# Transposing x for the attention of blocks 1 to 4 through DRAM scratch and VectorE instead of on TensorE, in a one-core Macaron layer

## The reference

```
x = x + 0.5 * ffn(layernorm(x))      # FFN 1
x = x + attention(layernorm(x))
x = x + 0.5 * ffn(layernorm(x))      # FFN 2

ffn(z):  z_prev = z shifted by one token in its sequence
         r = sigmoid((mu_r*z + (1-mu_r)*z_prev) @ W_r.T)
         k = (mu_k*z + (1-mu_k)*z_prev) @ W_k.T
         return r * (square(relu(k)) @ W_v.T)
attention(z): q = relu(z@Wq.T)/4; k = relu(z@Wk.T)/4; v = z@Wv.T; u = silu(z@Wu.T)
         per head: kv = k.T @ v over the whole sequence; o = q @ kv
         return (rmsnorm_per_head(o) * u) @ Wo.T
```

## Time and profile before

| | |
|---|---|
| median of the runs | 307.89 us |
| the profiled execution | 307.94 us, of which the span of the trace is 306.2 us (1.74 us lie outside) |
| PE busy | 298.5 us, 97% of the span |
| DVE, ACT, POOL busy | 81%, 77%, 70% |
| granted clock of PE | full in all 40 slices |
| DMA | 15.05 MB; 17122 of 28416 packets under 512 B |

### The profile page before, as it was taken

The page is one execution under the profiler, slowest core; times in us unless marked ns, Lnnn a source line. Parts: engine busy times, 40 slices in busy tenths (PEclk is TensorE's granted clock), DMA queues, the critical chain, the costliest instruction groups (busy, mean ns, idle before and its releaser), DMA issues.

```text
span 306.2 us, 5777 instructions
## 1 busy us (share of the span) xinstructions
PE 298.5 (97%) x2003; PEld 271.7 (89%) x2003; DVE 247.4 (81%) x601; ACT 235.5 (77%) x461; POOL 214.5 (70%) x237
## 2 busy tenths in 40 slices
PE   6999999999999999999999999999999999999995
PEld 4888879978988898998988998999999999999894
DVE  4899896677876966985993798596989798999695
ACT  3988949969779779689178368489797979699981
POOL 4598969779689489479168116736797979759823
PEclk9999999999999999999999999999999999999999
DMA  7950070070330510000000000000001101001123
GB/s 234 382 208 2 2 137 2 2 137 0 58 83 0 80 59 0 2 1 2 0 2 1 2 0 0 2 2 2 0 16 56 37 34 54 17 2 68 42 99 137
DMA packets 28416, 15.05 MB, mean 49 GB/s; under 512 B 17122, under 2 KB 27364, under 8 KB 28388
## 3 DMA queue, kind: packets, MB, share of 16 engines
q1 hardware_dynamic: 28096, 14.42, 16.7%
q10 hardware_dynamic: 292, 0.26, 0.2%
HBM read 8.39 MB, written 6.29 MB: 48 GB/s over the span
## 4 chain that ended last, share of the span: by engine, by line
PE 63%; DVE 16%; POOL 8%; ACT 7%; issue 3%; DMA 1%; ACTq 0%; DVEq 0%; POOLq 0%
PE psK L1328 6%; PE psX L1328 6%; PE psK L1330 6%; PE psK L1329 6%; PE psX L1330 6%; PE psX L1329 6%; PE psRV L1328 5%; PE psRV L1330 5%; PE psRV L1329 5%; DVE mix L978 3%; PE psA L1533 2%; PE psX L1546 2%; PE psK L1533 2%; PE psA L1345 2%; DVE gate L1054 2%
## 5 line engine op out<-in xcount | busy, mean ns | idle before, releaser
L978 DVE SCALAR_TENSOR_TENSOR mix<-psA,mu,mix 128x512 f32<-128x512 f32 x60 | 41.5, 744 | 10.0 <-ACT mix L663 10.0
L454 POOL TENSOR_TENSOR mix_k_lo<-mix,mix_k_hi 128x512 fp32r<-128x512 f32 x26 | 33.6, 1313 | 5.1 <-ACT mix_k_hi L696 5.1
L663 ACT ACTIVATE mix<-psA,one_mu 128x511 f32<-128x511 f32 x60 | 36.9, 697 | 0.0
L1328 PE MATMUL psRV<-ffn_hi,mix_r_hi 128*128 128x256 f32 x120 | 34.3, 286 | 0.0
L1330 PE MATMUL psRV<-ffn_hi,mix_r_lo 128*128 128x256 f32 x120 | 33.6, 280 | 0.0
L1329 PE MATMUL psRV<-ffn_lo,mix_r_hi 128*128 128x256 f32 x120 | 33.5, 279 | 0.0
L646 ACT ACTIVATE xn<-xs,shiftA,rstdA 128x256 f32<-128x256 f32 x53 | 27.9, 623 | 2.6 <-POOL shiftA L438 2.6
L1328 PE MATMUL psRV<-ffn_hi,act_hi 128*128 128x256 f32 x96 | 27.6, 287 | 0.2 <-POOL act_lo L476 0.2
L1330 PE MATMUL psRV<-ffn_hi,act_lo 128*128 128x256 f32 x96 | 26.8, 279 | 0.0
L1329 PE MATMUL psRV<-ffn_lo,act_hi 128*128 128x256 f32 x96 | 26.8, 279 | 0.0
L947 DVE BATCH_NORM_STATS2 statsA<-xs 128x6 f32<-128x256 f32 x64 | 22.4, 412 | 2.7 <-DMA xs<-x_dram 2.6
(11 more groups left out here) (211 smaller groups left out, 1086.5 us busy)
## 6 DMA issues: line engine op xcount, KB each, us to landing
xs<-x_dram SPq DMA_DIRECT2D x7, 512.0 KB, 7.8
out_dram<-xs SPq DMA_DIRECT2D x7, 512.0 KB, 2.8
spread<-xn SPq DMA_DIRECT2D x8, 256.0 KB, 4.5
squares<-spread SPq DMA_DIRECT2D x8, 256.0 KB, 2.7
out_dram<-xs SPq DMA_DIRECT2D x4, 128.0 KB, 1.7
xs<-x_dram ACTq DMA_DIRECT2D x2, 128.0 KB, 3.1
xs<-x_dram SPq DMA_DIRECT2D x2, 128.0 KB, 2.8
silu_u<-w_ffn_k_dram SPq DMA_DIRECT2D x1, 256.0 KB, 4.0
```

What stands on the lines that cost most here:

```text
L454: nc.gpsimd.tensor_tensor(mix_k_lo[:, h, :], mix[:, 0, h, :], mix_k_hi[:, h, :].bitcast(F32), ALU.subtract).then_inc(s_lo_k, 1)
L663: nc.scalar.activation(mix[:, rk, h, 1:BLOCK], psA[:, h, 0:BLOCK - 1], ACT.Copy, scale=one_mu[:, rk, h:h + 1]).then_inc(s_prev, 1)
L978: nc.vector.scalar_tensor_tensor(out=m, in0=psA[:, h, :], scalar=mu[:, rk, h:h + 1], in1=m, op0=ALU.mult, op1=ALU.add).then_inc(s_mix, 1)
L1328: nc.tensor.matmul(dst, a_hi, b_hi, start=start, stop=False)
```

## The change

Four things, all in stages 1 to 6:

1. The transposes of x for attention blocks 1 to 4 (`TURNED_X`) leave PE. SP stores x after FFN 1 from `xs` to a second scratch `spread_x` in pieces of 32 floats, loads it into `gout` (free at that time), and DVE turns it with `turn_x` into psX. The xn store now writes pieces of 128 floats, since ACT writes xn with the 32x32 blocks already in the scratch's order.
2. ACT does `x2_high(a)` between the two halves of `activate_k(i)` in stages 2 to 5. PE's `k_and_u` waits for each half of x2 by itself.
3. `stats_a` of blocks 5 to 7 moves one stage ahead: its four bn_stats stand before the four silus, and its bn_aggr behind `stats_b`. `keep_g` stands before `r_low`.
4. In stage 1 ACT squares act_k's second half instead of POOL; in stage 2 the split of wo stands a little earlier on POOL and ACT.

```diff
+        TURNED_X = range(1, 5)
+        quads_x = gout[:].rearrange("p t d -> p (t d)")
+        spread_x = nc.dram_tensor("spread_x", [len(TURNED_X), 2, QUADS, P, P], F32).ap()
...
-            for k, n in enumerate(TURNED):
+            for k, (n, a) in enumerate(zip(TURNED, TURNED_X)):
                 for g in range(2):
+                    sp.wait_ge(s_x1, 2 * a + g + 1)
+                    sp.dma_start(spread_x[k, g].rearrange("j p (q f) -> p q j f", f=QUAD),
+                                 row(xs, a, g * BANK, BANK).rearrange("p (q j f) -> p q j f", j=QUADS, f=QUAD)
+                                 ).then_inc(s_spread_x[g], 16)
+
                     sp.wait_ge(*normalized(n, 2 * g + 1))
-                    sp.dma_start(spread[k, g].rearrange("j p (q f) -> p q j f", f=QUAD),
-                                 xn[:, 2 * g:2 * g + 2, :].rearrange("p t (h j f) -> p (t h) j f", h=HALVES, j=QUADS)
+                    sp.dma_start(spread[k, g].rearrange("j p e -> p j e"),
+                                 xn[:, 2 * g:2 * g + 2, :].rearrange("p t d -> p (t d)").rearrange("p (j e) -> p j e", j=QUADS)
                                  ).then_inc(s_spread[g], 16)
                 if k > 0:
+                    sp.wait_ge(s_tB, 2 * a)
                     sp.wait_ge(s_tA, 2 * n)
                 for g in range(2):
+                    sp.wait_ge(s_spread_x[g], 16 * (k + 1))
+                    sp.dma_start(quads_x[:, g * BANK:(g + 1) * BANK],
+                                 spread_x[k, g].rearrange("j (c i) e -> (j c) (i e)", i=QUADS)).then_inc(s_quads_x[g], 16)
                     sp.wait_ge(s_spread[g], 16 * (k + 1))
...
-                activate_k(i)
-                if a is not None and i > 1:
+                if a in TURNED_X:
+                    activate_k(i, (0,))
+                    x2_high(a)
+                    activate_k(i, (1,))
+                else:
+                    activate_k(i)
+                if i > 5:
                     x2_high(a)
...
+            def turn_x(a):
+
+                dve.wait_ge(s_relu_q, 2 * a)
+                blocks = quads_x.rearrange("p (g i t h f) -> p g h t i f", g=2, i=QUADS, t=2, h=HALVES)
+                for g in range(2):
+                    dve.wait_ge(s_quads_x[g], 16 * (a - TURNED_X[0] + 1))
+                    for h in range(HALVES):
+                        last = nc.vector.transpose(
+                            psX[:, h, half(g)].rearrange("p (t c i) -> p t i c", t=2, i=QUADS), blocks[:, g, h, :, :, :])
+                        if g == 1:
+                            last.then_inc(s_tB, 1)
...
             for i in range(1, 7):
+                if i == 2:
+                    stats_a(4)
                 if 1 < i <= 5:
-                    stats_a(i + 2)
                     turn(i + 1, {4: [(s_wcen, 4)], 5: [(s_kvbd, 1)]}.get(i, ()))
+                if i - 1 in TURNED_X:
+                    turn_x(i - 1)
...
-                            pe.wait_ge(s_x2hi, 2 * a + HALVES)
-                            pe.wait_ge(s_x2lo, 2 * a + HALVES)
+                            pe.wait_ge(s_x2hi, 2 * a + c + 1)
+                            pe.wait_ge(s_x2lo, 2 * a + c + 1)
...
                 ffn_k(i, [(s_gacc, i - 1)])
-                transpose_b(i - 1)
                 ffn_r(i)
```

More of the change, by code:

```diff
@@ L170, in macaron @@
         s_quads = [sem(f"s_quads_{g}") for g in range(2)]
+        s_spread_x = [sem(f"s_spread_x_{g}") for g in range(2)]
+        s_quads_x = [sem(f"s_quads_x_{g}") for g in range(2)]
         s_prev = sem("s_prev")
@@ L465, in act_squares @@
                 for h in range(HALVES):
+                    if (n, h) == (1, 1):
+                        continue
                     pool.wait_ge(s_act_hi, parts(n) + h + 1)
@@ L566, in _ @@
                     kt_low(i - 1)
+                if i == 2:
+                    pool.wait_ge(s_wo_hi, 1)
+                    nc.gpsimd.tensor_tensor(wo_lo[:], wo[:], wo_hi[:].bitcast(F32), ALU.subtract).then_inc(s_wo_lo, 1)
                 scales_b(i)
@@ L645, in normalize @@
                         continue
-                    nc.scalar.activation(xn[:, t, :], tile_row(xs, b, t), ACT.Identity,
+                    given, rows = tile_row(xs, b, t), xn[:, t, :]
+                    if n in TURNED:
+                        given, rows = given.rearrange("p (h j f) -> p h j f", h=HALVES, j=QUADS), spread_rows(t)
+                    nc.scalar.activation(rows, given, ACT.Identity,
                                          bias=shiftA[:, t:t + 1], scale=rstdA[:, t:t + 1]).then_inc(s_xn, 1)
@@ L713, in activate_k @@
                     nc.scalar.activation(act_hi[:, h, :], act_k[:, h, :], ACT.Square).then_inc(s_act_hi, 1)
+                    if (n, h) == (1, 1):
+                        act.wait_ge(s_act_hi, HALVES)
+                        nc.scalar.activation(act_k[:, h, :], act_k[:, h, :], ACT.Square).then_inc(s_act_first, 1)
             def activate_k2(n):
@@ L848, in _ @@
                     nc.scalar.activation(wo_hi[:], wo[:], ACT.Identity).then_inc(s_wo_hi, 1)
+                x1_high(i)
                 relu_q(i - 1)
@@ L1220, in _, with projections @@
             ffn_weight_low(2)
-            def projections(a):
+            def projections(a, n=None):
                 for t in range(TILES):
+                    if n is not None:
+                        bn_rows(n, (t,))
                     silu(a, t)
             for i in range(1, 7):
+                if i == 2:
+                    stats_a(4)
                 if 1 < i <= 5:
-                    stats_a(i + 2)
                     turn(i + 1, {4: [(s_wcen, 4)], 5: [(s_kvbd, 1)]}.get(i, ()))
+                if i - 1 in TURNED_X:
+                    turn_x(i - 1)
                 if i > 1:
@@ L1234, in _ @@
                     stats_a(3)
-                projections(i - 1)
+                projections(i - 1, i + 3 if 2 <= i <= 4 else None)
                 if i == 6:
@@ L1244, in _ @@
                 stats_b(i)
+                if 2 <= i <= 4:
+                    bn_all(i + 3)
+                keep_g(i - 1)
                 r_low(i + 1)
@@ L1247, in _ @@
                     center_weight("v", 4)
-                keep_g(i - 1)
                 if i == 4:
@@ L1627, in _ @@
             ffn_k(5, [(s_gacc, 4)])
-            transpose_b(4)
             ffn_r(5)
```

11 lines of the change are left out of this document (6 added, 5 removed).

## The result

The changed kernel takes 326.2 us (median of four runs, 324.28 to 327.31) beside 307.97 us for the kernel before on the same chip: a ratio of 1.0559 [1.0516, 1.0601], 5.6% slower. The profiled execution has a span of 324.7 us. The direction was as forecast, the size was not: 317.0 us was predicted, and 326.2 lies above the range.

A forecast was written before the change was run, and what follows sets the result against it. PE, busy 97% of the span, bounds the kernel; its 4.7 us saving lies inside the wait for x. Span 306.2 plus 9.1 (x 6.5 late, k_lo 2.6) is 315.3, with 1.74 outside 317.0 us; range 310.3 to 322.5.

The forecast's parts named there:

- T: The moment x after FFN 1 of a block is complete, at the end of the second add_ffn1.
- L: Way from T through store and load to the last load's landing: 7.6 us, bounds 6.0 to 9.4.
- 2.06 + 1.72 + 11.8: Loop after L: DVE's transposes 2.06 us, ACT to the column of previous 1.72, from there to the next T 11.8.
- then the load takes 2.7 us: Last step of L: the load behind the store lands 2.7 us later.
- the queue chokes: Rival: small-piece stores hold SP, L is 9 us or more, result 322 us and up; chance 0.02 beyond 9.4.
- T of stage 1: Start of the sum: T in stage 1 falls at 40.2 us, 40.61 before the change.
- Three turns: Three rounds from T to T at 23.2 us each, bringing stage 4's T to 109.8 us.
- T of stage 4 to k_and_u of stage 5: From T in stage 4 to the start of stage 5's k_and_u: 10.7 us, reaching 120.5.
- The wait for k_lo: In stage 5 POOL's k_lo comes 2.6 us late for gram; longer turns hide this in stages 2 to 4.
- Only POOL is late: Rival: x2 in time, act_hi's half 1 1.0 us later behind x2_high, k_lo eats 0.8 us a stage; 307 us; chance 0.06.
- PE keeps its gain: Rival: PE stays the bound in the stages and keeps its saving; 303.2 us, some 304; chance 0.10.
- keep_g ahead of r_low: Removes PE's stop for g_acc and smaller ones at other stages' ends; 1.0 us together.

The follow-up runs named there:

- e4: e3 plus all stores and loads of x through DRAM, which nobody uses until long after; 311.6 us.
- e8: e3 plus the stores of x, without any load of x; 307.9 us.
- e13: Changed kernel without the loads of x; its stores and all orders stay, and DVE turns whatever lies in gout; 319.8 us.
- e5: Changed kernel without stores and loads of x, and with ACT's old order (both halves of activate_k, then x2_high); 305.9 us.
- e2: Changed kernel without the stores and loads of x; DVE's transposes and ACT's new order stay; 311.6 us.
- e7: e1 with loads issued x, x, xn, xn and DVE's turn_x ahead of turn(i+1); 311.1 us.
- e3: Changed kernel with PE transposing x again, no x through DRAM and ACT's old order; the other edits stay; 306.6 us.
- e1: Changed kernel with ACT's old order: x2_high behind both halves of activate_k; 322.2 us.
- e6: Changed kernel with ACT writing xn in its old layout and the xn store in pieces of 32 floats; 329.5 us.
- e10: e1 with DVE's turn_x ahead of turn(i+1), load order as in the changed kernel; 313.2 us.
- e11: e1 with loads issued x, x, xn, xn, DVE's order as in the changed kernel; 323.5 us.
- e9: e3 with xn's old layout and the xn store in pieces of 32 floats; 307.0 us.
- e12: e7 with ACT's new order, x2_high between the halves of activate_k; 314.3 us.

## Why the prediction was right in kind and wrong in size

**Right: which resource would set the time.** The forecast said that all that PE saves lies inside a wait for x, and that this wait stands in ACT's program and closes a loop through the next T. The chain of after is that loop. A turn is L + 15.6 us by the forecast's steps (2.06 + 1.72 + 11.8); measured, the turns of 24.8, 25.6 and 24.9 us less their L of 9.1, 9.9 and 9.25 leave 15.7, 15.7 and 15.65. PE does stop 3.08, 1.52 and 2.32 us before k_and_u in stages 2 to 4 (not in stage 5, where a stop was forecast, too).

**Wrong: the step "then the load takes 2.7 us" in L.** SP's queue in stage 3's turn, beside the earlier trace rows:

```profile
66.57 1.59 SPq L405 DMA_DIRECT2D spread<-xn  x1
68.29 0.45 SPq L413 DMA_DIRECT2D gout<-spread_x  x1
...
70.54 0.32 SPq L416 DMA_DIRECT2D squares<-spread  x1
```

The last load is issued at 70.54 and landed at 75.82, with three loads of the same size ahead of it, the first 2.25 us earlier. Issue (0.67 us to the last store's, forecast 0.65) and store (3.96, forecast 4.25) were right or better; the load was 5.28, and 4.40 and 4.62 in the other two turns. I had priced the neighbours of the stores and left the loads at the median of a trace that never had more than two in the queue. The range's long end (9.4) had the same fault. Of the rival "the queue chokes" the length came true, L of 9 or more, and I gave such times 5% (0.03 and 0.02); its mechanism did not, for the last store was issued 0.67 us after T, where 0.65 was forecast. e4, e8 and e13 show by themselves that adding the loads of x costs the time, e4 and e8 on a kernel that does not even use them.

How a queue of four makes the last load slow is only half answered. Windows of after from the issue of that load on, and the queue of instruction transfers in the half microsecond from 72.50 (packets, MB, share of 16 engines):

```profile
70.54:73.50 2.96, 2.96 (x15) 2.45 (x14) 1.45 (x4) 1.28 (x3) 2.96 (x2) 1.00 0.87 269
73.50:75.80 2.30, 2.30 (x17) 2.11 (x16) 0.00 (x0) 1.15 (x2) 1.15 (x2) 1.00 0.04 9
```

```profile
q8 instruction: 1, 0.02, 22.3%
```

In the last 2.3 us before the load lands the DMA engines are nearly idle (share 0.04, 9 GB/s). Just before that, between 72.50 and 73.00, a transfer of instructions of 16 KB (queue q8) has started. Such a transfer starts inside each of the slow last loads of after; in the fourth trip, where that load took 3.46 us, it starts only 0.3 us before the landing. Over all 15 traces 27 of the 184 loads of `squares` and `gout` took over 4.4 us, and every one has such a transfer starting inside it, among them three with at most one more load in the queue (5.16 us in e5, 4.93 in e13's third trip, 4.44 in e8). The 87 loads without one took 2.8 us (median) and 4.36 at most. No run moved these transfers, so that they cause the delay is not shown, and how L's excess divides between them and the queue stays open.

**The sum, term by term** (spans, 324.7 measured and 315.3 forecast, 9.4 apart):
- T of stage 1, 41.13 for 40.2: 0.9. It belongs to the start-up, which is 1.3 us later in this trace than in that of before and as early as there in that of e13.
- Three turns, 75.3 for 69.6: 5.7. L accounts for 5.4 of it.
- T of stage 4 to k_and_u of stage 5, 12.5 for 10.7: 1.8. Here x was in time. turn(i+1) waits in this stage for kv_bd, which comes behind kv(0) and so behind the late gram (DVE's kv_bd 123.57, its transposes 124.03), and PE reached k_and_u without an idle. I had taken it that k_lo's lateness in stages 2 to 4 is hidden by the longer turns; in stage 4 it is not.
- From there to the end, 195.8 for 194.8: 1.0. In stage 5 gram starts 138.31 - 128.93 = 9.4 us behind k_and_u, where it was 8.3, and runs 5.22 us for 2.82: together 3.5 us late, where 2.6 were forecast. The wait for k_lo was priced, the clock behind it not.

**Half right: the rivals.** "Only POOL is late" was priced at the 0.8 us per stage that PE gains. e2 shows the mechanism with x in time: 5.6 us (e2 less e5), more than all that PE gained, since act_hi's second half was queued not only behind 1.0 us of x2_high but behind the transposes of psA and psX that x2_high waits for. "PE keeps its gain" would need trips of no length, and e5, which has none, gains 0.7 to 2.5 us of the 3.2 in the runs and nothing in the stages of its trace. So the transposes were not worth the whole 0.79 us a stage that the issue distance says: in e5's trace POOL's k_lo and once xn's load take their place.

**Right: the rest.** keep_g ahead of r_low was given 1.0 us and measures 1.05. The Trainium skill's "VectorE: DVE Perf Modes", "Rules for kernel authors", would leave 128x128 transposes on TensorE; here DVE's way gains at most a little when the trips cost nothing (e5), and with trips its best order still costs over 4 us (e7 beside e3). The runs agree with the rule.

## What to carry to other kernels

Price a new transfer by where it stands in the queue: the last of four loads took 3.5 to 5.3 us where loads took 2.7 before, and a load that nobody waits for delayed the one that somebody did. In an engine's program, look at what stands behind the new wait, and put the wait that is needed first in front: two lines of DVE's program swapped gave back 9 us, nearly three times the 3.2 us of the transposes. An engine at 97% is not proof that a us off it is a us won; an experiment that grants the new path for nothing (here: turning whatever lies in the buffer) shows about the most that the new path can bring.

## What the runs showed of the hardware that I had not expected

**PE's clock.** The granted clock was full in all 40 slices before. In the stages of after, e1, e2, e6, e7, e10, e11 and e13 it falls to 1.2 GHz, and each time PE stands idle or has just done so; in those of e3, e4, e5, e8, e9 and e12 it stays full. Windows of gram in stages 2 and 5 of after, which follow stops of PE for k_lo of 1.82 and 0.95 us and have another of 0.65 us inside:

```profile
63.81:69.11 5.30, 4.66 (x24) 4.45 (x25) 4.01 (x15) 2.40 (x5) 4.06 (x5) 0.68 0.86 160
...
138.31:143.53 5.22, 4.56 (x24) 4.36 (x25) 3.75 (x11) 1.86 (x4) 2.75 (x3) 0.70 0.02 5
```

The 24 matmuls take 5.3 and 5.2 us there (5.2 in stage 4, too). In stage 3 they take 3.82 us, with a stop of the same kind inside but at full clock, so some 1.4 us are the clock's. In e1 the drop comes in the first half of k_and_u. Its first and last such window:

```profile
54.97:60.02 5.05, 5.05 (x13) 3.95 (x13) 4.23 (x9) 4.85 (x10) 2.07 (x3) 0.53 0.00 0
...
128.76:131.61 2.85, 2.85 (x12) 2.33 (x13) 2.40 (x4) 2.85 (x6) 1.36 (x3) 1.00 0.00 0
```

The same twelve matmuls take 5.05 and 2.85 us. PE had stood idle 4.00 us before the first and 2.57 before the last, but the length of that idle alone does not decide: in e7 idles of 1.78 us were followed by clocks of 0.69 and 0.61, and one of 2.23 us by 1.00; in e10 3.31 us was followed by 1.00. What does decide stays open. A wait of PE here cost its own length and, often but not always, 1.1 to 2.4 us more (k_and_u's first half takes 3.98 to 5.26 us, the longest in e6 and e11, instead of 2.85).

**SP's issue.** The second xn store of a turn, in pieces of 128 (128x4x128), holds SP 1.59 us, where stores in pieces of 32 held it 0.67 and 1.02 before. The larger pieces are not the reason: in e2, with the same xn stores and no x stores before them, each holds SP 0.37 us and lands in 2.2 us, while in e9, with pieces of 32 and no x stores, they hold it 0.59 to 1.83 us and land in 3.4 to 5.2. It is behind the x stores, in pieces of 32, that the xn store holds SP longer (0.99 us behind the first, 1.59 behind the second).
